# Cross-attention and quantised FFN on one core: where the biases of q and k are added

## What is computed

```python
q = _ln((x @ Wq + bq).reshape(b, s1, H, HD), qn_w, qn_b)          # per-head layer norm
kv = concatenate([y_main @ Wk + bk, y_main @ Wv + bv], axis=-1)   # heads take k and v in turn
k = _ln(kv[..., :HD], kn_w, kn_b)
ctx = attn(q, k, v) + attn(q, k_dca, v_dca)                       # softmax over 112 and over 16 keys
x = x + ctx @ Wo + bo
x = x + ffn(layernorm(x))                                         # fake-quantised, relu
```

## Time and profile before

| | us |
|---|---|
| three runs | 419.50, 421.99, 416.52 |
| median | 419.5 |
| profiled execution | 418.69 |
| its span | 416.9 |

### The profile page before, as it was taken

The page is one execution under the profiler, slowest core; times in us unless marked ns, Lnnn a source line. Parts: engine busy times, 40 slices in busy tenths (PEclk is TensorE's granted clock), DMA queues, the critical chain, the costliest instruction groups (busy, mean ns, idle before and its releaser), DMA issues.

```text
span 416.9 us, 7653 instructions
## 1 busy us (share of the span) xinstructions
PE 337.5 (81%) x2353; PEld 269.1 (65%) x2383; DVE 326.0 (78%) x829; ACT 212.2 (51%) x390; POOL 186.2 (45%) x271
## 2 busy tenths in 40 slices
PE   1165797778998999997989999999899999898721
PEld 0033654566777777876877878777677778687510
DVE  5667746689696989896889899989798997947342
ACT  0205752534656575755565756657474757533311
POOL 8503211230737273645273645545454637363532
PEclk9996889998999999998999999999999999959665
DMA  7940053340817171727081716354435526170001
GB/s 223 343 137 0 1 155 115 102 117 0 202 42 194 38 209 38 206 57 187 28 217 41 205 61 184 98 146 123 122 105 140 134 73 173 48 192 2 25 25 50
DMA packets 32867, 47.53 MB, mean 114 GB/s; under 512 B 9272, under 2 KB 19772, under 8 KB 32828
## 3 DMA queue, kind: packets, MB, share of 16 engines
q1 hardware_dynamic: 31296, 45.64, 39.3%
q10 hardware_dynamic: 1532, 1.42, 1.1%
HBM read 33.93 MB, written 13.11 MB: 113 GB/s over the span
## 4 chain that ended last, share of the span: by engine, by line
PE 38%; DVE 24%; issue 15%; DMA 12%; SPq 4%; POOL 2%; ACT 2%; ACTq 2%; DVEq 0%; POOLq 0%
PE bank L1134 15%; PE bank L1244 7%; DMA q_stack<-stack_scratch 6%; DVE neg_max L950 4%; DMA wd_raw<-in_L_xattn_Wkv_dca 3%; PE bank L1355 3%; PE bank L1213 3%; DVE wq_raw L1011 2%; ACTq L553 2%; SPq L358 2%; SPq L362 2%; PE bank L1366 2%; DMA stack_scratch<-k_lo 1%; PE bank L1224 1%; DVE wq_raw L1054 1%
## 5 line engine op out<-in xcount | busy, mean ns | idle before, releaser
L1244 PE MATMUL bank<-v_aug,prob_store 128*128 128x66 f32 x512 | 70.0, 282 | 7.0 <-DVE seg_out L963 4.6
L1244 PEld LDWEIGHTS bank<-v_aug,prob_store 128*128 128x128 f32 x512 | 66.1, 199 | 8.5 <-issue 6.0
L461 POOL TENSOR_TENSOR k_lo<-wkv_raw,k_hi 128x448 f16<-128x448 f32 x16 | 17.2, 1073 | 115.7 <-issue 115.5
L950 DVE TENSOR_REDUCE neg_max<-bank 128x4 f32<-128x448 f32 (+1 forms) x128 | 45.1, 414 | 12.6 <-PE bank L1213 12.5
L648 ACT ACTIVATE prob_store<-bank,exp_scale 128x512 f32<-128x512 f32 x64 | 42.2, 685 | 24.5 <-PE bank L1225 23.9
L659 ACT ACTIVATE wkv_raw<-bank,affine 128x448 f32<-128x448 f32 (+1 forms) x32 | 22.5, 748 | 44.8 <-PE bank L1284 44.1
L476 POOL TENSOR_TENSOR finals<-seg_out 128x128 f32<-128x128 f32 x64 | 29.1, 456 | 26.5 <-DVE seg_out L963 24.4
L1224 PE MATMUL bank<-q_stack,k_stack 128*128 128x128 f16 x256 | 34.7, 223 | 1.4 <-ACT maxT L549 1.4
L1134 PE MATMUL bank<-wq_hi,xT_hi 128*128 128x512 f32 x64 | 30.7, 480 | 4.8 <-DVE xT_lo L974 4.8
L1225 PE MATMUL bank<-maxT,sel 128*128 128x128 bf16 x256 | 34.5, 222 | 0.0
L1213 PE MATMUL bank<-k_stack,q_stack 128*128 128x128 f16 x256 | 20.8, 225 | 13.0 <-issue 8.8
(11 more groups left out here) (197 smaller groups left out, 911.8 us busy)
## 6 DMA issues: line engine op xcount, KB each, us to landing
k_stack<-stack_scratch SPq DMA_DIRECT2D x32, 256.0 KB, 3.9
q_stack<-stack_scratch SPq DMA_DIRECT2D x64, 128.0 KB, 4.1
x_in<-in_x SPq DMA_DIRECT2D x16, 256.0 KB, 4.3
out<-finals SPq DMA_DIRECT2D x16, 256.0 KB, 4.2
y_in<-in_ctx SPq DMA_DIRECT2D x16, 128.0 KB, 4.2
stack_scratch<-k_hi SPq DMA_DIRECT2D x16, 128.0 KB, 1.7
stack_scratch<-k_lo SPq DMA_DIRECT2D x16, 128.0 KB, 1.9
stack_scratch<-q_hi SPq DMA_DIRECT2D x16, 128.0 KB, 1.8
```

Source lines behind the costliest of these rows:

```text
L461: g.tensor_tensor(lo[:, :, 0:keys], blocks(n)[:, :, 0:keys], hi[:, :, 0:keys], ALU.subtract).then_inc(done.sem, 1)
L950: v.tensor_reduce(neg_max[:, HG * gr:HG * (gr + 1), seg], s4[:, :, lo:hi], AX.X, ALU.max, negate=True).then_inc(max_ready.sem, 1)
L1244: last = mm(bank[6 + gr % 2][:, VW * h:VW * (h + 1)], probs[:, gr % 2, h], v_aug[:, Bt.parity, HG * gr + h], start=True, stop=True)
```

## The change

The two bias matmuls at the end of the k and q products (L1138) are gone. In the first live step of stage A, PE multiplies `ones3` by `bias_split` once for each bias, into banks 1 and 7 (`setup_biases`), and ACT copies the two results to `bias_full` in SBUF. In every step POOL adds these to k_raw and q_raw in place, after ACT has copied them from PSUM. ACT's square of k waits for the sum and stands behind the fourth exponential instead of ahead of the third; the square of q waits for its sum at its old place. The sum x_plus moves on POOL from ahead of combine(0) to the end of the step. The tiles ident16 and bo_row are dropped; bo is loaded to out_bias directly.

```diff
+            def setup_biases():
+                pe.wait_ge(bias_split_ready.sem, 48)
+                pe.wait_ge(ydcaT_copied.sem, 1)
+                for n, to in ((1, bank[1]), (0, bank[7])):
+                    mm(to[:, :], ones3[:], bias_split[:, n], start=True, stop=True).then_inc(bias_made.sem, 1)
...
-                if bias is not None and chunks[-1] == end:
-                    last = mm(dst, ones3[:, 0:m], bias, start=False, stop=True)
...
                     if A.first():
+                        setup_biases()
                         setup_keys()
...
                     if A.first():
+                        for n, made in ((1, bank[1]), (0, bank[7])):
+                            act.wait_ge(bias_made.sem, 2 - n)
+                            copy(bias_full[:, n], made[:, :]).then_inc(bias_copied.sem, 1)
...
-                if A is not None:
-                    act.wait_ge(*kraw_ready.of(A))
...
                 if Bt is not None:
                     expo(3)
+                if A is not None:
+                    act.wait_ge(*ksum_ready.of(A))
...
+                    s.activation(k_sq[0:MAIN], k_raw[0:MAIN, A.parity], ACT.Square).then_inc(ksq_ready.sem, 1)
...
-                    act.wait_ge(*qraw_ready.of(A))
+                    act.wait_ge(*qsum_ready.of(A))
...
-                if Bt is not None:
-                    if Bt.first():
-                        pool.wait_ge(out_bias_ready.sem, 1)
-                    pool.wait_ge(*xres_loaded.of(Bt))
-                    if Bt.has(1):
-                        pool.wait_ge(*x1_ready.of(Bt.back(1)))
-                    g.tensor_tensor(x_plus, x_res[Bt.parity], out_bias[:], ALU.add).then_inc(xplus_ready.sem, 1)
+                if A is not None:
+                    if A.first():
+                        pool.wait_ge(bias_copied.sem, 2)
+                    pool.wait_ge(*kraw_ready.of(A))
+                    g.tensor_tensor(k_raw[0:MAIN, A.parity], k_raw[0:MAIN, A.parity], bias_full[0:MAIN, 1], ALU.add
+                                    ).then_inc(ksum_ready.sem, 1)
+                    pool.wait_ge(*qraw_ready.of(A))
+                    g.tensor_tensor(q_raw[:, A.parity], q_raw[:, A.parity], bias_full[:, 0], ALU.add
+                                    ).then_inc(qsum_ready.sem, 1)
...
                 if Bt is not None:
                     combine(2)
                     combine(3)
+                if Bt is not None:
...
+                    g.tensor_tensor(x_plus, x_res[Bt.parity], out_bias[:], ALU.add).then_inc(xplus_ready.sem, 1)
```

More of the change, by code:

```diff
@@ L33, in first, with second @@
         return self.reg is None and self.const == 0
+    def second(self):
+        return self.reg is None and self.const == 1
     def index(self):
@@ L315, in _ @@
             load(fb_in, fb_row[:], row(ffn_bias))
-            load(bo_in, bo_row[:], row(bo))
+            load(bo_in, out_bias[:], row(bo))
             dca_rows = dca_scratch.rearrange("(b r) n -> b r n", r=DCA)
@@ L539, in step @@
                     combine(3)
+                if Bt is not None:
+                    if Bt.first():
+                        pool.wait_ge(out_bias_ready.sem, 1)
+                    pool.wait_ge(*xres_loaded.of(Bt))
+                    if Bt.has(1):
+                        pool.wait_ge(*x1_ready.of(Bt.back(1)))
+                    g.tensor_tensor(x_plus, x_res[Bt.parity], out_bias[:], ALU.add).then_inc(xplus_ready.sem, 1)
             run(pool, step, {-2: setup_rows})
@@ L736, in step @@
                     expo(3)
+                if A is not None:
+                    act.wait_ge(*ksum_ready.of(A))
+                    if A.first():
+                        act.wait_ge(wklo_ready.sem, 2)
+                        act.wait_ge(wvlo_ready.sem, 2)
+                    if A.has(1):
+                        act.wait_ge(*kss_ready.of(A.back(1)))
+                    s.activation(k_sq[0:MAIN], k_raw[0:MAIN, A.parity], ACT.Square).then_inc(ksq_ready.sem, 1)
                 if C is not None:
@@ L900, in setup_output @@
                 dve.wait_ge(bo_in.sem, 16)
[L901 removed]
+                v.tensor_tensor(out_bias[:], bank[7][:, :], out_bias[:], ALU.add).then_inc(out_bias_ready.sem, 1)
             def setup_ffn():
@@ L1125, in _, with split_product @@
             mm, tr = nc.tensor.matmul, nc.tensor.transpose
-            def split_product(dst, xT_h, xT_l, w_h, w_l, chunks, bias, m):
+            def split_product(dst, xT_h, xT_l, w_h, w_l, chunks, m):
                 first = chunks[0] == 0
@@ L1134, in split_product @@
                         last = mm(dst, a[:, c, 0:m], w[:, c, :], start=first,
-                                  stop=bias is None and c == end and a is xT_l)
+                                  stop=c == end and a is xT_l)
                         first = False
-                if bias is not None and chunks[-1] == end:
-                    last = mm(dst, ones3[:, 0:m], bias, start=False, stop=True)
                 return last
-            pe.wait_ge(idents_made.sem, 3)
+            pe.wait_ge(idents_made.sem, 2)
             def setup_transposed():
@@ L1253, in step @@
                     pe.wait_ge(*y_loaded.of(A))
+                    if A.second():
+                        pe.wait_ge(bias_copied.sem, 2)
                     for c in range(YC):
@@ L1274, in step @@
                     pe.wait_ge(*clo_ready.of(C))
-                    split_product(bank[7][:, :], cT_hi, cT_lo, wo_hi, wo_lo, range(XC), None, P
+                    split_product(bank[7][:, :], cT_hi, cT_lo, wo_hi, wo_lo, range(XC), P
                                   ).then_inc(attn_ready.sem, 1)
@@ L1317, in step @@
                         pe.wait_ge(*qn_ready.of(N))
-                    split_product(bank[2][:, :], xT_hi, xT_lo, wq_hi, wq_lo, range(XC // 2), bias_split[:, 0], P)
+                    split_product(bank[2][:, :], xT_hi, xT_lo, wq_hi, wq_lo, range(XC // 2), P)
                 if Bt is not None:
```

26 lines of the change are left out of this document (13 added, 13 removed).

## The result

The changed kernel took 424.97 us (median of 5, 421.08 to 428.31), the kernel before 416.52 us (414.13 to 421.99) beside it: ratio 1.0185, 95% interval 1.0109 to 1.0261.

What follows compares the result with a forecast made beforehand. It took a DVE–PE ring through L990, L939 and seg_out(0) as the bound. Steady part +6.5 and fill with drain +0.5 made +7.0 us: 425.7 from the profiled 418.69, 426.5 from the median, stated as 426, range 414 to 434.

Steps and rivals of the forecast that it cites:

- What bounds: Steady step: DVE from the maxima through L990 and L939 to seg_out(0), then PE from `weigh(2)` to the next scores.
- (a): PE before `weigh(2)`: two bias matmuls gone, 0.46 us a step, worth 0 in the steady part.
- R1: Rival: POOL's second add goes ahead of the waiting L939, +9 to +13 us more, about 437 us; chance 0.10.
- (b): POOL's two adds, 1.27 us each: first shuts out L939 as x_plus did, 0 us; second follows L939.
- (c): POOL behind the adds: combine(3) ends at about 255.78 instead of 255.68; PE's context transpose 0.1 us later, hidden.
- (d): ACT squares k after the fourth exponential: 0 us, at most 0.07; a DVE wait for ksum through it would refute this.
- (e): x_plus behind combine(3) delays L485 on POOL, so L990 on DVE waits: 0.8 us a step, bounds 0.3 and 0.96.
- side estimate: POOL adds at 1.07 us by the GPSIMD page: L990's delay 0.6 us a step, total some 1.7 us smaller.
- The sum: Whole kernel: steady part +6.5 us; fill and drain together +0.5; total +7.0 us.
- the three late steps: Three steady steps where scores come so late that L990 falls after L485: 0 us added.
- R2: Rival: PE is the bound and the lock costs nothing, so removing the matmuls gains 6.9 us: 412 us; chance 0.11.
- R3: Rival: matmul gain and lock cost both absorbed because scores wait for q_stack: 418 to 421 us; chance 0.19.

Runs made afterwards that it cites:

- The kernel with the slot: Kernel before, with x_plus alone moved on POOL behind the next step's k_hi and k_lo copies, after DVE's k and q scaling: 417.9 us, ratio 1.004.
- the first trace: Profiled execution of the changed kernel, nothing further altered: 428.31 us, span 426.5 us.
- The second run: Changed kernel once more, unaltered, against the kernel before: 426.5 us, ratio 1.025; its trace has a span of 424.8 us.

## Why the prediction was right

It said 426.0, within 414 to 434; the two measurements are 425.0 and 426.5 us. Point by point:

- **What bounds: wrong.** The ring "DVE from the maxima ... L939, up to seg_out of group 0; then PE from `weigh(2)`" is not the one that binds. The kernel with the slot took the whole stall of L939 away and gained no time (0.999 to 1.008); q_lo moved alone moved the time both ways. The failing step was to count PE's waits by the engine they name: the wait of 0.29 us for q_stack was seen and counted as DVE's, like the 0.39 us for seg_out, and the ring was closed through seg_out. The last wait ahead of the maxima is the one that counts, and it is q_stack's: the scores start 0.09 us after its last landing in every steady step. The drawn ring was a second chain 0.1 to 0.3 us behind, and L990 lies on both; that the forecast survived is luck as far as this step goes.
- **(a) right.** Worth 0, for the reason that they lie outside the ring; measured -0.3%, interval -0.6 to +0.1%. What I did not see is that they also decide when q_raw is there, and so whether R1 happens.
- **(b) right.** L957 at 1.89 us, and the second add, whose record of 1.74 us holds its wait for L957. The row of L1073 gave the right order here, but as a rule it is not safe: the kernel with the matmuls kept shows the other order, at 438.8 us where R1 said about 437.
- **(c), (d) nearly right.** The wait of DVE's sum over k for the square, which the prediction named as the sign that (d) is wrong, is there: 0.15 to 0.24 us in six of the steady steps of the first trace, 1.02 us in one step at each end of it. In the step shown it is 0.15, and combine(3) ends at 262.93, 0.05 us after x_plus's record begins: no gap is left on POOL there. With q_lo early the adds are no longer free (about 4 us, from two intervals that just overlap).
- **(e) right in mechanism and place, a little large in size.** Forecast 1.0 us for L990 in the steady steps; measured in the first trace 0.95, 1.20, 0.94, 0.40, 0.85, 1.08 and 0.91. Over all steps L1008's stretch beyond 0.17 us is 6.5 us, that of before 0.7: 5.8 us more, where the sum had 6.4 and 0.5. By the rule of the Trainium skill (SBUF — State Buffer, § Who interferes with whom), that whoever issues first keeps the shared ports for its whole instruction, both stalls follow; the traces agree, L1008 starting 0.26 us behind L490 waits 0.9 us. Which of two waiting instructions comes next is another matter, and the spans of 424.8 and 436.6 us of the kernels with either order differ mostly by that. The prediction's side estimate with 1.07 us an add takes 0.2 us off (e) for one GpSimd instruction, but x_plus and L490 both have that form: 0.4 us a step would go, about 3 us in all. The measured records are 1.27 to 1.30 us, and the forecast did not rest on it.
- **The sum, right by luck: two errors cancel.** Cut where the forecast cuts, at the first and the last of L990's meetings with L485 (136.10 and 356.57 us before), it said +0.7 for the fill, +6.5 for the steady part and -0.2 for the drain. The second run (span 424.8, so 7.9 more than before, 7.0 said) has +3.1, +4.4 and +0.5; the first trace (span 426.5) has +7.1, +2.7 and -0.1. The fill was put too small by 2.4 us or more; the lower clock at the out-bias matmuls alone is 2.6, and what makes the rest of the 7.1 us stays open. The steady part was put too large: an ordinary step is 0.7 longer, where 0.8 was said, but the step with a late landing that took 23.1 us before took 20.33 in both traces of the changed kernel. The prediction priced the three late steps at zero. That late landings hide part of the stall fits these traces; how much of it is the change and how much the luck of one execution, three traces don't say.
- **Rivals.** R2 fell: PE is not the bound, with the matmuls left out (416.1 us). R3 fell as a forecast (418 to 421 us), though its mechanism, the wait for q_stack, is the ring. R1 did not happen here and happened one edit away.

## What to carry to other kernels

Cut the chain of waits to one steady step and see whether it closes on itself: what is in the loop costs, and a stall that is not in it (here 1.1 us on 1.86 in every step) is worth next to nothing until the loop is shortened. Check the joins of the chain against the order of the program: here one ended a transfer 0.76 us before its last landing. Then move one instruction of the loop each way and compare the slopes; an advance that is cut off shows how near the next chain is. Where GpSimd and VectorE shut each other out, an edit elsewhere that shifts a copy by 0.3 us can go with another order, so two queued GpSimd instructions beside a waiting VectorE one are a risk even where the trace shows the good order. One thing is left untried: four of SP's six loads do not read q_lo, stand behind its put in the program, and take 2.2 us of issue in the ring (248.43 to 250.61).

## What the runs showed of the hardware

- Of two GpSimd adds and one waiting VectorE instruction, either order occurs: 1.9 us (40 steps) or 3.1 us (10 steps) for an instruction that takes 0.74 us alone, and it goes with whether the second add's input was ready when the first began.
- A VectorE tensor_scalar on 128x32 f32, 0.17 us alone, takes up to 1.23 us beside a 1.3 us GpSimd instruction with two inputs.
- The path from q_lo's put to the scores costs 7.3 us (248.00 to 255.32): the put, six loads issued in turn from 248.43 to 251.54, 4.1 us from the issue of the last one to its landing, and 0.09 us from there to the first matmul.
- The granted clock at one place of the fill was 1.00 in seven kernels and 0.50 in seven others, after about equal work and pauses in the microseconds ahead; the out-bias matmuls took 3.67 us in the seven and 5.2 to 6.4 us in the others.
